# Sparse graph attention on one core: ten places of its own for a target's keys in place of eleven

## What is computed

```
q = (ht @ Wq + bq).reshape(T, H, HD) / sqrt(HD)
k = (hs @ Wk + bk).reshape(S, H, HD)
v = (hs @ Wv + bv).reshape(S, H, HD)
logits = where(edge_mask != 0, einsum('thd,shd->hts', q, k), -1e30)
ctx = einsum('hts,shd->thd', softmax(logits), v).reshape(T, D)
ht = layer_norm(ht + ctx @ Wo + bo)
out = x + ht + gelu(ht @ W1) @ W2
```

| S | smallest of the 16 tiles | mean | largest |
|---|---|---|---|
| 9 | 95 | 142 | 177 |
| 10 | 54 | 91 | 116 |
| 11 | 32 | 55 | 72 |

## Time and profile before

### The profile page before, as it was taken

The page is one execution under the profiler, slowest core; times in us unless marked ns, Lnnn a source line. Parts: engine busy times, 40 slices in busy tenths (PEclk is TensorE's granted clock), DMA queues, the critical chain, the costliest instruction groups (busy, mean ns, idle before and its releaser), DMA issues.

```text
span 393.9 us, 5345 instructions
## 1 busy us (share of the span) xinstructions
PE 337.4 (86%) x1654; PEld 280.3 (71%) x1654; DVE 300.6 (76%) x678; ACT 170.1 (43%) x407; POOL 238.8 (61%) x303
## 2 busy tenths in 40 slices
PE   3999988427742959999899999999999989999984
PEld 1688877226532648887688778788887878888873
DVE  5977894598915989889889998999999595762210
ACT  4999664301303244716343571653435245243210
POOL 6654047777777777787777778777777771200100
PEclk9999999859695869999999999999999999999998
DMA  7996977778878565756666583646447351101000
GB/s 231 298 272 202 254 253 248 228 263 238 197 246 235 141 185 139 217 126 179 184 190 173 138 241 106 188 131 196 136 129 236 94 171 47 41 0 53 2 27 31
DMA packets 31158, 65.64 MB, mean 167 GB/s; under 512 B 5370, under 2 KB 15894, under 8 KB 31128
## 3 DMA queue, kind: packets, MB, share of 16 engines
q0 software_dynamic: 17696, 49.27, 46.0%
q1 hardware_dynamic: 13408, 15.99, 12.0%
q10 hardware_dynamic: 24, 0.01, 0.0%
HBM read 76.82 MB, written 6.29 MB: 211 GB/s over the span
## 4 chain that ended last, share of the span: by engine, by line
POOL 28%; PE 28%; DVE 22%; issue 13%; DMA 6%; ACT 1%; POOLq 1%; DVEq 0%; ACTq 0%
POOL near L540 25%; DVE logits L1119 7%; PE turned L1534 6%; DMA near<-kv_saved,far_index 5%; PE wide L1520 5%; PE lines L1476 4%; PE lines L1351 3%; PE turned L1352 3%; DVE near L1108 2%; PE small L1398 1%; POOL rstd_y L485 1%; PE wide L1325 1%; PE turned L1497 1%; DVE stats L862 1%; DVE values L1137 1%
## 5 line engine op out<-in xcount | busy, mean ns | idle before, releaser
L540 POOL DMA_INDIRECT near<-kv_saved,index x176 | 177.0, 1006 | 56.5 <-issue 54.4
L1476 PE MATMUL lines<-values,ident 128*128 128x264 f32 x352 | 86.0, 403 | 9.2 <-DVE values L1137 8.1
L1476 PEld LDWEIGHTS lines<-values,ident 128*128 128x128 f32 x352 | 68.8, 199 | 23.5 <-issue 11.6
L1520 PE MATMUL wide<-yT,w 128*128 128x256 f32 x256 | 61.0, 389 | 0.0
L1534 PE MATMUL turned<-w,hidden 128*128 128x256 f32 x256 | 58.5, 382 | 2.2 <-DVE result L1160 1.9
L1108 DVE TENSOR_TENSOR near<-near,lines 128x2816 f32<-128x2816 f32 x16 | 49.3, 3079 | 10.3 <-DMA near<-kv_saved,index 10.3
L1137 DVE TENSOR_TENSOR values<-near,small 128x3072 f32<-128x3072 f32 x16 | 53.6, 3350 | 2.5 <-ACT small L723 2.5
L1534 PEld LDWEIGHTS turned<-w,hidden 128*128 128x128 f32 x256 | 47.5, 190 | 10.4 <-DVE result L1160 4.5
L1119 DVE TENSOR_REDUCE logits<-near 128x96 f32<-128x3072 f32 x16 | 53.6, 3353 | 0.0
L1520 PEld LDWEIGHTS wide<-yT,w 128*128 128x128 f32 x256 | 48.8, 195 | 6.3
L736 ACT ACTIVATE context<-lines,sums_inverse 128x32 f32<-128x32 f32 x128 | 24.6, 307 | 54.1 <-DVE sums_inverse L1144 54.1
(11 more groups left out here) (148 smaller groups left out, 527.8 us busy)
## 6 DMA issues: line engine op xcount, KB each, us to landing
adjacency<-in_adj POOLq DMA_DIRECT2D x16, 512.0 KB, 7.5
kv_saved<-kv_out SPq DMA_DIRECT2D x3, 1024.0 KB, 6.5
near<-kv_saved,index POOLq DMA_INDIRECT x176, 3.7
ht<-in_L_gnn_h_target SPq DMA_DIRECT2D x4, 512.0 KB, 18.2
w<-in_L_gnn_W SPq DMA_DIRECT2D x2, 1024.0 KB, 8.7
xr<-in_x SPq DMA_DIRECT2D x8, 256.0 KB, 4.6
out<-result SPq DMA_DIRECT2D x8, 256.0 KB, 3.3
xs<-in_x SPq DMA_DIRECT2D x3, 512.0 KB, 6.9
```

The lines of the kernel that those rows point to most:

```text
L540: pool.indirect_dma_start(out=near[:, n % RING, s, :], out_offset=None, in_=kv_saved, in_offset=bass.IndirectOffsetOnAxis(ap=ids.bitcast(U ...
L1476: pe.matmul(acc, ident[:], values[:, s, :], start=(s == 0), stop=False)
L1520: mm = pe.matmul(wide[:, f % 2, half * 2 * P:(half + 1) * 2 * P], w1[:, d, fs], yT[:, e % 2, d, :], start=(d == 0), stop=(d == DC - 1))
```

## The change

```diff
--- before.py
+++ after.py
@@ -28,7 +28,7 @@
-SLOTS = 11
+SLOTS = 10
 KEYS = 24
 REST = KEYS - SLOTS
 OFF, WHO, END = KEYS, KEYS + 1, KEYS + 2
```

## The result

The kernel with ten places takes 379.08 us, the median of four runs (378.37 to 379.93), beside 394.49 us (394.04 to 395.02) for the kernel before: a ratio of 0.961, with a 95% interval of 0.9581 to 0.9638, or 15.4 us less. The forecast was 378.0 us, with 374.0 to 383.0 as its range. The profiled execution took 378.37 us, with a span of 376.7.

What follows compares the result with a forecast made beforehand. POOL's gather queue bounds up to tile 3, then POOL, DVE and PE nearly equally, PE at the end; 14.1 + 2.0 - 0.4 + 1.35 = 17.0, less 0.5, is 16.5 us: from 394.51 to 378.0 us, range 374.0 to 383.0.

Steps and rivals of the forecast that it cites:

- DVE alone sets the pace: Rival, chance 0.12: only DVE's own 12.8 us come off, giving 381.7 us.
- POOL alone: Rival, chance 0.10: the whole 20.8 us of POOL's 16 removed gathers is gained, giving 373.7 us.
- PE takes over: Rival, chance 0.22: after 154 us PE binds and only 0.45 us per tile is gained, giving 382.1 us.
- To tile 3: First stage, POOL alone late: far gathers 2 and 3 come 5.2 and 6.5 us earlier, tile 4 starts 7.0 us earlier.
- Tiles 4 to 11: Middle four pairs, POOL, DVE and PE nearly equal: gains of 1.8, 2.3, 1.7 and 1.3 us, together 7.1.
- the root, and with it the odd far gather, waits for words and statistics: Coupling in the middle pairs: these are made in the even round; DVE reaches the odd far gather within 0.5 us of landing.
- Far landings: Far gather carries on average 91 rows in place of 55: growth between nothing and 2.3 us, taken as 0.4.
- Tiles 12 to 15 and the end: Last stage: far 13 gains 2.0 us more, less 0.4 for landing; PE's three remaining sums give 1.35 us.
- 0.5 taken off by judgement: Deduction from the sum of 17.0 us for PE's small waits in saturated pairs, leaving 16.5 us.
- the sign named for PE's rival: Sign that the forecast is wrong: pairs above 33.8 us with PE never idle.
- Slower, by the general path: Rival, chance 0.02: one tile's surplus above the shared place's 128 partitions starts the general path, costing over 1100 us.
- Every second tile would be over: Claim that with nine places every second tile's surplus would exceed the shared place's 128 partitions.

Runs made afterwards that it cites:

- E1: Kernel after the change with an eleventh near gather per tile put back, its rows unread: 393.07 us, 0.998 of the kernel before.
- E4: Kernel before the change less the eleventh near gather alone, DVE and PE still working on twelve places: 384.54 us, 0.9763 of the kernel before.
- E2: Kernel after the change with DVE's three wide instructions over one more place, of zeros: 383.29 us, 0.9736 of the kernel before.
- E3: Kernel after the change with an eleventh product with the identity per tile on PE, over zeros: 380.54 us, 0.9652 of the kernel before.
- E8: Kernel after the change with all 128 rows of each far gather filled: 469.5 us, where the kernel before took 474.9 us beside it.
- E12: Kernel with nine places (SLOTS = 9) in place of ten: 3991.99 us in one run, beside 393.29 us for the kernel before.

## Why the forecast was right, and where it was off

**What bounds.** Right, in its main step: that POOL's queue, 61% busy by the page, is the late one up to tile 3, and one of three near-equal engines behind it. E1 and E4 show it from both sides. "DVE alone sets the pace" is out: by occupancy, which the Trainium skill (Perfetto Trace Analysis, "Identifying the Most-Contended Engine") takes for the engines but PE, DVE leads POOL with 76% to 61%, yet DVE's work back costs 5 us (E2) and the gather back 14.7 us (E1, 393.07 against 0.961 x 393.75 = 378.4). The 0.3 us between gathers is not in POOL's occupancy. "POOL alone" is out too: E4 is 384.5, not 374. "PE takes over" is out as a whole, as E3 is at 0.9652 and not 0.9765, but holds in the first pair.

**To tile 3.** Forecast 5.2 and 6.5 us for far 2 and far 3, measured 6.4 and 7.4. The gathers gave the 5.2 and 6.5; the first gather went out 0.5 us earlier in this execution (55.04 for 55.55), and far 2 landed 4.35 us after its start (112.16 to 116.51) instead of 5.0. Tile 4's score is 8.0 us earlier, forecast 7.0.

**Tiles 4 to 11.** This is the term that was mis-sized. Forecast gains of 1.8, 2.3, 1.7 and 1.3, measured 0.8, 2.7, 0.5 and 1.3: 5.3 instead of 7.1 us. The need of PE was taken from the last pair, 32.8 us, and used for all. By the earlier trace rows PE was busy for 34.36 us of the first pair, 33.5 less its 0.9, and it is busy for 34.2 of 34.4 after: work beyond the sums fell into that window. The chain runs over PE without a break from tile 3's sums at 144.1 to the words at 160.8, and E3 adds its whole 0.9 to that pair. The coupling "the root, and with it the odd far gather, waits for words and statistics" was named, but what it leads to wasn't: with POOL early, it is PE's words that time POOL. In the third pair, far 9 took 1.1 us longer to land than before. E3, with PE's product back and the same rows, has that pair at 33.2 us and far 9 landed in 3.6 us at most, so the loss lies in this landing and not in PE. POOL also stands 1.2 us longer than usual ahead of near 9 (199.72), for which the trace names no releaser; it does so in E2, E3 and E4 too, so that isn't the loss.

**Far landings.** Taken as 0.4 us more. The table has the time from the start of the instruction to the end of DVE's wait, in us. Counted on the inputs, the far gather's rows grow with the change from 72 to 116 at tile 9 and by 40, 22 and 49 at tiles 13 to 15 (on average from 54 to 90, where the prediction has 55 and 91); E1 and E3 have as many as the kernel after.

| | tile 9 | tile 13 | tile 14 | tile 15 |
|---|---|---|---|---|
| before | 3.45 | 3.31 | 2.70 | 3.26 |
| after | 4.58 | 3.42 | 3.20 | 3.39 |
| E1 | 4.89 | 3.32 | 3.26 | 3.33 |
| E3 | 3.61 at most | 3.40 | 3.28 | 3.52 |

The four landings of the kernel after are 0.47 longer on average, but over 1 us of that is tile 9's alone, which lies between 3.6 and 4.9 with the same rows. The three others are 0.25 longer. The fit of the Trainium skill (DMA: Bandwidth & Descriptors, "Anatomy of one DMA") gives an estimated 0.2 for these rows. The trace agrees in size, at tiles 13 to 15 and in E8, but what grew does not follow the rows (0.50 for 22, 0.11 for 40). What makes a single landing 1 us longer stays open.

**Tiles 12 to 15 and the end.** Far 13 is 14.7 us earlier, forecast 15.7. The three sums behind it gave 1.5 (4.45, 4.53 and 4.45 us where 4.96, 5.13 and 4.89 stood), and DVE's last result comes at 372.06 instead of 388.52, 16.5 us earlier; the forecast had 16.5 to 17.0. The span gains 17.2, as the last store, too, took 0.7 us less.

**The number.** The medians differ by 15.4 us, forecast 16.5. The profiled execution of before was 1.1 us over its median and that of after is the lowest of its four runs, so the profiles make the gain look 1.8 us larger than it is. That the sum comes so close is in part luck. Up to DVE's last result the profiles have 8.0 + 5.3 + 1.4 + 1.8 = 16.5 us, where the forecast had 7.0 + 7.1 + 1.6 + 1.35, less 0.5 taken off by judgement: the middle was 1.8 us too good, and an early stage that gained 1.0 us more, an end that gained 0.4 more and the 0.5 made up for it.

**The signs.** Of those that the prediction named, most came: 160 and 16 gathers 1.30 us apart, the lengths of L1108, L1119 and L1137, the scores of tiles 4 and 12 within 1 us, the waits for "DVE index", no `slow_` instruction. Three did not. DVE's wait for far 2 is 11.2 us and not above 12, since DVE, too, is 4.8 us earlier there. Two of the four middle pairs, 34.4 and 33.9 us, lie above 33.4. And the first of them, with PE idle for 0.2 us, is the sign named for PE's rival.

**Slower, by the general path.** It didn't run. Its point was right: 116 keys are below 128, 177 are above (E12). Its price, a lower bound, was a third of the real one. "Every second tile would be over" was too low: with nine places 12 of the 16 tiles are.

## What to carry to other kernels

Read a queue of small DMAs by the distance from start to start, not by busy share: here 1.30 us per gather made an engine at 61% the one that others waited for. When several engines are within a few per cent of each other, removing work from one pays only until the next is met, so price each stretch with each engine's own need in that stretch, and take a change that relieves all of them at once: the parts gave 9.2 us (gather, E4) and 0.7 us (DVE and PE, E1) alone, and 15.4 together. And a capacity with a slow path behind it is a cliff: one place fewer again would have won another 12 us in the fast part and cost 3600.

## What was not expected of the hardware

The time of a gather's instruction on POOL hardly depends on how many of its rows are valid: the 176 near gathers of the kernel before lie between 0.99 and 1.20 us with a median of 1.00, from the first tiles, where all 128 rows are valid, to the last places of later tiles, where most are empty. E12's 144, without the emptiest places of the others, take 1.007 us on average. So a place costs POOL its full 1.30 us even when few of its rows are filled, and that is what made the eleventh one dear.
